# A sum ahead of gathers, and two normalisations moved from VectorE to GpSimd, in a fused four-block model on one core

## What is computed

```python
x = _layernorm(x + L0_attn(x))   # a state space mixer
x = _layernorm(x + L0_ffn(x))    # 64 experts, 8 chosen for each token
x = _layernorm(x + L1_attn(x))   # attention, 16 heads of 8 features
x = _layernorm(x + L1_ffn(x))    # three dense layers with weights of +1 and -1

def _layernorm(x, axis=-1, eps=1e-05):
    m = jnp.mean(x, axis=axis, keepdims=True)
    v = jnp.var(x, axis=axis, keepdims=True)
    return (x - m) / jnp.sqrt(v + eps)
```

## Time and profile before

| | us |
|---|---|
| median of 3 runs | 670.5 (669.43 to 671.48) |
| the profiled execution | 670.14 |
| its span in the profile | 668.4 |
| busy: PE / VectorE / ScalarE / GpSimd | 594.4 / 480.3 / 395.3 / 372.0 |
| groups 3 to 8 of the attention, about | 409 to 501 |

### The profile page before, as it was taken

How to read it: one execution, slowest core, us unless ns; L and a number is a source line. 1 busy time by engine, 2 the same in 40 slices (tenths; PEclk the granted TensorE clock), 3 DMA queues, 4 the chain that set the end, 5 groups by cost and what they waited for, 6 DMA issues and landing times.

```text
span 668.4 us, 13071 instructions
## 1 busy us (share of the span) xinstructions
PE 594.4 (89%) x3696; PEld 371.4 (56%) x3697; DVE 480.3 (72%) x1226; ACT 395.3 (59%) x896; POOL 372.0 (56%) x398
## 2 busy tenths in 40 slices
PE   3973999879999999999886999799989999888994
PEld 2252666659999999999761333233323234344552
DVE  5469743555556656778679788788878886869886
ACT  3411454326666666667657877467777778866541
POOL 6321777777777217775707787887746000235652
PEclk9976799989999999999986999899999999999998
DMA  5999951136777668887454254125203200000001
GB/s 173 434 370 221 399 184 52 52 126 193 225 221 223 197 173 226 224 219 196 131 180 112 70 158 107 42 89 146 53 31 107 71 2 2 1 0 1 17 17 31
DMA packets 98998, 91.51 MB, mean 137 GB/s; under 512 B 10707, under 2 KB 84531, under 8 KB 98739
## 3 DMA queue, kind: packets, MB, share of 16 engines
q1 hardware_dynamic: 91275, 75.24, 37.0%
q0 software_dynamic: 7680, 15.74, 8.3%
HBM read 44.87 MB, written 45.61 MB: 135 GB/s over the span
## 4 chain that ended last, share of the span: by engine, by line
PE 57%; DVE 12%; POOL 10%; DMA 7%; issue 5%; SPq 4%; ACT 3%; POOLq 0%; DVEq 0%; ACTq 0%
PE ps L1472 11%; PE ps L1459 8%; PE ps L1587 6%; PE ps L1577 6%; DMA arena<-zeros 6%; POOL arena L533 4%; PE ps L1567 4%; PE ps L1467 4%; PE ps L1482 4%; PE ps L1384 3%; PE ps L1389 3%; SPq L348 2%; DVE mx L1136 2%; DVE arena L1254 2%; DVE arena L1246 1%
## 5 line engine op out<-in xcount | busy, mean ns | idle before, releaser
L1136 DVE TENSOR_REDUCE mx<-ps 128x2 f32<-128x1024 f32 x128 | 150.9, 1218 | 29.2 <-PE ps L1567 28.6
L748 ACT ACTIVATE big<-ps 128x512 f32<-128x512 f32 x256 | 141.1, 597 | 41.3 <-PE ps L1577 38.6
L521 POOL DMA_INDIRECT xd<-xt,idx x120 | 120.1, 1001 | 49.4 <-issue 35.6
L1472 PE MATMUL ps<-arena,xbT 128*128 x496 | 97.2, 319 | 4.0 <-DVE xbT L1062 4.0
L533 POOL DMA_INDIRECT big<-od,idx x72 | 71.4, 992 | 49.4 <-DMA od<-big 25.0
L1577 PE MATMUL ps<-arena 128*128 128x512 bf16 (+1 forms) x256 | 85.9, 388 | 5.6 <-ACT big L748 4.5
L1058 DVE TENSOR_TENSOR hm<-sg,ps 128x176 f32<-128x176 f32 x124 | 41.8, 337 | 67.0 <-ACT sg L687 65.4
L1567 PE MATMUL ps<-arena 125*128 125x512 bf16 (+1 forms) x256 | 71.8, 394 | 9.2 <-DVE mx L1136 9.0
L1472 PEld LDWEIGHTS ps<-arena,xbT 128*128 128x128 f32 x496 | 76.2, 194 | 4.9 <-issue 4.8
L1459 PE MATMUL ps<-arena,hmT 96*128 x496 | 77.4, 279 | 1.1 <-ACT hmT L683 1.1
L677 ACT ACTIVATE big<-ps 128x256 f32<-128x256 f32 x124 | 47.7, 384 | 47.8 <-PE ps L1459 47.6
(11 more groups left out here) (219 smaller groups left out, 994.3 us busy)
## 6 DMA issues: line engine op xcount, KB each, us to landing
big<-xd SPq DMA_DIRECT2D x62, 256.0 KB
od<-big SPq DMA_DIRECT2D x62, 256.0 KB
arena<-scr SPq DMA_DIRECT2D x96, 96.0 KB
xd<-zeros SPq DMA_DIRECT2D x1, 8192.0 KB, 60.5
xd<-zeros SPq DMA_DIRECT2D x1, 7680.0 KB, 21.9
arena<-w_gu SPq DMA_DIRECT2D x1, 5632.0 KB
scr<-places SPq DMA_DIRECT2D x8, 384.0 KB, 2.8
arena<-w_d SPq DMA_DIRECT2D x1, 2560.0 KB
```

The source lines that it names most:

```text
L521: pool.indirect_dma_start(out=xd[f], out_offset=bass.IndirectOffsetOnAxis(ap=idx[:, t, k:k + 1], axis=0), in_=xt[:, t], in_offset=None).th ...
L748: act.activation(ering[:, HG * (mt % 2) + h], ps[:, 4 + h % 2, :], ACT.Exp, scale=SCALE).then_inc(exp_ready, 1)
L1136: v.tensor_reduce(mx[:, k, TB * h + 2 * a:TB * h + 2 * a + 2], ps[:, 2 * a:2 * a + 2, :], AX_X, ALU.max).then_inc(s1_free, 1)
L1472: ins = pe.matmul(ps[:, 2 + (u - GU) % 2, I2 * a:I2 * a + I2], xbT[:, (u - GU) % 2, a], wgu_s[:, bass.ds(expert(2 * (u - GU) + a), 1), :]. ...
```

## The change

Three edits, all on the LayerNorm of sequences 2 and 3 ahead of the attention:

- For t = 12 GpSimd sums tile 11 ahead of tile 12's gathers instead of behind them.
- The root of sequence 2 moves from behind the second gather of tile 13 to behind the fourth gather of tile 12.
- The four normalising instructions of sequence 2 and of sequence 3 move from VectorE's queue (groups 4 and 8) to GpSimd's, directly behind the root. The new `normalise` on GpSimd waits for `s_rstd` and increments `s_xn`, as VectorE's did.

```diff
+            def normalise(k):
+
+                q = k % B
+                pool.wait_ge(s_rstd, k + 1)
+                for t in range(TB * q, TB * q + TB):
+                    ins = pool.tensor_scalar(xt[:, t], tmp[:, t], mv[:, t, 0:1], rstd[:, t:t + 1], ALU.subtract, ALU.mult)
+                ins.then_inc(s_xn, 1)
+
...
             for t in range(FIRST[1] + 1, NT):
-                bring(1, t, back_slot(t), 0, 2)
-                if t == 3 * TB + 1:
+                if t == 3 * TB:
+                    sum_rows(t - 1)
+                bring(1, t, back_slot(t), 0, 4)
+                if t == 3 * TB:
                     rstd_of(2 * B + 2)
-                bring(1, t, back_slot(t), 2, TOP_K)
-                sum_rows(t - 1)
+                    normalise(2 * B + 2)
+                bring(1, t, back_slot(t), 4, TOP_K)
+                if t != 3 * TB:
+                    sum_rows(t - 1)
             sum_rows(NT - 1)
...
             rstd_of(2 * B + 3)
+            normalise(2 * B + 3)
             qk_parts(3)
...
                         if isinstance(i, int):
-                            if (h, a) == (0, 1) and i in TURN_IN and i:
-                                normalise(xt, tmp, 2 * B + TURN_IN[i])
```

## The result

| | before | after |
|---|---|---|
| median of 5 runs, us | 670.36 (669.43 to 671.48) | 680.68 (678.48 to 682.12) |
| ratio, 95% interval | | 1.0156 (1.0137 to 1.0174) |
| profiled execution / its span, us | 670.14 / 668.4 | 678.48 / 676.7 |

The change makes the kernel 10.3 us slower. The prediction said 4.3 us slower, with a range that ended at 677.3.

What follows compares the result with a forecast made beforehand. GpSimd's full queue was taken to bound the kernel, making tile 15's sum hold up sequence 3: 3.1 us for its later turn plus 1.6 of low clock gave +4.7, 674.8 us, range 671.3 to 677.3.

Steps and rivals of the forecast that it cites:

- late gather: Tile 15's second gather on GpSimd: its lateness, seen beside an instruction fetch, comes again, 1.8 us.
- named signs: Included sequence 2 turned near 427 at full clock, VectorE idle 7 us or more, GpSimd's last sum ending 484 to 487.
- Normalisation on GpSimd: Behind both roots: 0.44 us an instruction, between 0.32 and 0.55; four make 2.04 us.
- normalisation is dear: Rival, chance 0.07: beside VectorE's work each GpSimd normalising instruction takes 1 us; +9.1 us, 679.
- The low clock: PE behind group 8's stall: slower work at 1.2 GHz, +1.6 us, between nothing and 3.3.
- GpSimd's twelve gathers and tile 12's sum: GpSimd's queue from 427.4: gathers at 1.25 us each end at 442.1, the sum at 447.4.
- given back: GpSimd's queue: exchanging a restart and one slower sum of the old run gives a little time back.
- Group 4's gain: PE turns sequence 2 at 427.35 instead of 431.81, winning 4.45 us, plus 1.63 us from full clock.
- The way to group 8: Groups 5 to 7 run 6.1 us earlier; VectorE reaches sequence 3's statistics at 477.3.
- the gain is carried through: Rival, chance 0.08: GpSimd doesn't bound groups 5 to 7, or catches up; 664.0, or 667 with half the gain.
- A slip in the sum: GpSimd's queue: tile 15's sum was put at 484.5, before adding 1.8 us for its second gather.

Runs made afterwards that it cites:

- order_only: Kernel before with only the new order of tile 11's sum and sequence 2's root, VectorE still normalising both sequences: 674.57 us, ratio 1.0062.
- skip15: Changed kernel without the eight gathers of tile 15, whose sum adds what lies in the slot: 678.86 us.
- price run: Kernel before with 28 more GpSimd instructions, seven forms four times each, where nobody waits for GpSimd; the normalisation's form took 795 ns.
- dve15_b: Changed kernel with sequence 2's root behind tile 12's sixth gather, VectorE normalising both sequences and adding tile 15's rows: 675.04 us, ratio 1.0068.

## Why the prediction was right and wrong

**What bounds the kernel: right.** Tile 11's sum is 10.1 us earlier on the anchor's scale, turn 2 3.25 us earlier, GpSimd waits 2.54 us for the statistics (2.3 forecast), the late gather of tile 15 comes again with its 2.07 us, and VectorE's wait moves to sequence 3. order_only shows the loss of the gain, skip15 that tile 15's sum decides. Three of the named signs did not come: VectorE stood idle 6.02 us and not 7 or more, the last sum ended 93.20 us behind the anchor (488.6 on the scale of the kernel before, not 484 to 487), and turn 2 was not at full clock.

**The size: wrong by half.** From the anchor on the sum said +4.7 and the profile says +9.24. The step that failed is the size of three terms, the price of the normalisation on GpSimd first:

- *Normalisation on GpSimd* ("I take 0.44 in the middle"). It took 0.785 us, above the upper bound of 0.55, and that counts twice on the path: 3.14 - 2.04 = 1.1 us each time, so 2.2. The bound came from rows with bytes as input and one operation with a constant. The price run shows what no row had: a float32 input costs 3.34 ns an element in this form, against the 2.55 taken as the upper slope. The price for the simplest bodies in the Trainium skill (GPSIMD Engine Reference, Performance versus the Vector engine), weighed as near the lower bound of 0.32 us, was further off still. The rival "normalisation is dear" had the right mechanism with the wrong reason (it expected waiting beside VectorE). That its 679 lies near the measured time is partly luck: it took 1 us an instruction, too much, and the other two terms are missing from it.
- *The low clock* ("+1.6 us by the same comparison"). It cost 2.5 to 2.7. The row for 1.63 came from a shorter stall, whose low clock ended 3.6 us behind the turn (at 435.4); this one ended 5.4 us behind it (at 499.3). The upper bound of 3.3 held.
- *GpSimd's twelve gathers and tile 12's sum*: 15.3 and 5.7 us instead of 14.7 and 5.2, 1.1 us in all. I had priced them all by their undisturbed rows. The slow sum of tile 12 was not new: it took 5.76 us in the kernel before, and the prediction counted that as given back.
- *Group 4's gain* ("4.45 us" and "these 1.63 us should go too"). Turn 2 came 3.25 us earlier, since the normalisation was 1.1 us longer; with 1.95 us of idle PE ahead of it the turn took 1.09 us, at low clock again, and none of the 1.63 went. It changed nothing at the end: VectorE's wait for tile 15 was shorter by as much. order_only, with turn 2 at full clock, does get the 1.63 back.
- *The way to group 8* ("Groups 5 to 7 then run 6.1 us earlier", VectorE "arrives at its statistics of sequence 3 at 483.4 - 6.1 = 477.3"). PE's turning of outputs was 3.3 us earlier in group 4 and 1.4 in groups 5 to 7, and VectorE was done with `split_max` 0.8 us earlier. Tile 12's sum beside VectorE's splitting, for which the prediction has no term, took 1.9 us. As VectorE waited for tile 15 anyway, this shortened its wait and added nothing to the time. But the rival "the gain is carried through" was priced by the same 6.1 us (664.0), and skip15 shows that turn 3 would have come no earlier than before.
- *A slip in the sum*: 479.0 + 0.53 + 5.2 makes 484.7 and not 484.5 for tile 15, 0.2 us.
- *The late gather* ("while a fetch of instructions ran on its queue"). It came again as forecast, but without a fetch beside it: in the changed kernel the packet of q8 lies between 458 and 459, and GpSimd falls idle ahead of the late gather only at 466.3. Nor do the rows say whose queue q8 is. What makes the gather late stays open.

The first three make 4.4 of the 4.5 us that are missing. The last us between 9.3 and the 10.3 of the medians is within the scatter ahead of the anchor, which is up to 3 us.

**The range.** Its upper end, 677.3, held 0.9 us for a dearer price and 1.7 for a longer low clock. With the measured 2.2 for the price it would have reached 678.6, still under the measured 680.68; nothing in it stood for slower gathers and sums.

## What to carry to other kernels

Before moving work off one engine, look at what the receiving engine's queue sets next: here it was full for 130 us and its last sum had 0.75 us to spare, so what was put into it, waiting included, came out at the end less that slack (in order_only 2.5 us of waiting made turn 3 1.85 us later), and the time won at one meeting of the engines was lost at the next. A sum that is moved also comes beside other instructions: here it fell on VectorE's splitting and took over half of the gain before group 8 was reached. Price an operation on GpSimd only from a row with its own input type and its own scalars, or run it once by itself. A stall on PE can cost more than its length: in these kernels stalls of some 2 to 6 us were mostly followed by 1.0 to 2.5 us more at the low clock (skip15's 1.94 us in group 8 cost nothing).

## What the runs showed of the hardware

- On GpSimd a 128x128 float32 tensor-scalar with two operations and both scalars in SBUF takes 785 to 795 ns (3.34 ns an element and 0.37 us); VectorE does the same in 0.28 to 0.33 us (four take 1.10 in group 8 of the kernel before and 1.33 in group 4), and GpSimd's own tensor-tensor of that shape takes 0.46.
- VectorE's 128x512 operation with two SBUF inputs took 0.68 us while GpSimd only issued gathers, and 2.44 beside GpSimd's sum (dve15_b). A 128x512 cast, with one input, took 2.22 us beside it and 0.42 without it.
- Repeating matmuls in the idle time kept the granted clock at 1.00, worth 2.5 us in group 8 of the changed kernel and 1.6 in group 4 of the kernel before, each from the turn to the same later instruction.
- The second gather of tile 15 came 2.07 or 2.08 us behind the one ahead of it, instead of 0.30, in every profile here that issues it. A fetch of instructions lay beside it in the kernel before, and none in the changed one, where the nearest ends 7 us sooner. It was not tried to move it.
